# Post-norm Mamba layer with gated feed-forward on one core: mean and variance from channel halves, joined on GpSimd instead of VectorE

## The chip, the cores and the metric

The kernel runs on one core of a Trainium2 chip. Its time is the device time of one execution in microseconds (us); lower is better. The engines are TensorE (PE in the profile, its weight loads PEld), VectorE (DVE), ScalarE (ACT), GpSimd (POOL) and SyncE (SP, which only issues DMAs here).

## The reference

Input x is 8 sequences of 1024 tokens with 256 channels, in float32. One layer is computed, a Mamba block and then a gated feed-forward, each followed by a residual sum and a layer norm without weights:

```
def _layernorm(x, axis=-1, eps=1e-05):
    m = jnp.mean(x, axis=axis, keepdims=True)
    v = jnp.var(x, axis=axis, keepdims=True)
    return (x - m) / jnp.sqrt(v + eps)
...
    xz = jnp.einsum('bld,ed->ble', x, W_in); xi, z = jnp.split(xz, 2, axis=-1)
    u = silu(xc + conv_b)                       # xc: causal convolution of xi, 4 taps
    dt = softplus(W_dt of the first 16 rows of W_xproj u, plus b_dt)
    h = h * exp(dt A) + (dt * u) B;  y = sum over the 16 states of h C
    y = (y + u * D_skip) * silu(z);  out = W_out y
x = _layernorm(x + mamba(x))
x = _layernorm(x + w_down(silu(w_gate x) * (w_up x)))
```

The einsums of the feed-forward use int32 weights divided by 127. The middle lines are the reference's loops written short.

## The kernel before

**Chunks.** The tokens are handled in 16 chunks of 512 (two per sequence). The inner 512 channels are 4 blocks of 128 partitions, with 16 states each, so a chunk has 64 scans (`scan`, L846, VectorE), each over 512 tokens of one channel block and one state. The chunks overlap in a software pipeline: during the scans of chunk k the engines also do the input projection, convolution and `dt` of chunk k+1 ("head") and the output projection, first norm, feed-forward and second norm of chunk k-1 or k-2 ("tail"). Each engine has its own program. The side work is put between the scans by tables written out by hand, keyed by (quad of four scans, place in the quad): `PE_SIDE`, `ACT_SIDE`, `DVE_SIDE`, `POOL_SIDE`, and `*_LAST`, `*_END` for the last chunk. All order between engines comes from semaphores.

**What feeds the scans.** A scan reads a decay (ScalarE, `decay_step`, L641, into one of three PSUM banks) and a drive. GpSimd makes the drives: `drive_unit` (L512) multiplies `dtu` with two rows of B in one instruction of 128x1024 elements; a chunk has 32 such units, unit j feeds scans 2j and 2j+1, and there are four buffers, so unit j waits for the end of scan 2(j-4)+1 (L501). TensorE transposes the states of a finished quad (`transposes`, L1075), ScalarE copies them out (`evacuate`, L648), and TensorE sums over states (L1089).

**Side work that this case touches.**
- Convolution (`conv`, L867, VectorE): three instructions per channel block, each reads two SBUF tensors (`xi` and `acc`). Table entry (2, 2) does block 0, behind scan 10; entry (5, 0) does blocks 1 to 3 with the first half of the first norm's sums, `("r1", 0)`, ahead of the last two.
- `clamp` (L875, a one-input VectorE instruction on 128x1024) and `softplus_max` (L881, two SBUF inputs) make `dt`.
- `add_and_stats` (L883 to L896, VectorE), twice per norm and chunk: the residual sum, `bn_stats` for two blocks of 128 tokens, a wait for the first of these, a throwaway memset, and `bn_aggr` for the two blocks. The places are (5, 0) and (5, 2) for the first norm, (15, 1) and (15, 3) for the second.
- `scale_and_shift` (L545 to L554, GpSimd), once per norm and chunk: from `mv` it makes `rstd` and `shift`. Table items `("std", 0)` at (6, 1), behind drive unit 13, and `("std", 1)` at (0, 1), behind unit 1. Units 14 and 15, `gate_y` (L527) and `dt_times_u` (L543) stand behind the first.
- `normalise` (L707, ScalarE) waits for the fourth of these steps and applies both.
- `heads` (L532, GpSimd) waits for the last convolution of the chunk, ahead of units 12 and 13.
- Products of TensorE go through two PSUM banks in turn (`RING`, L166): `room` (L1115) makes a product wait until the product two before it has been read. In the feed-forward the readers are VectorE's `gate_silu` (L901) and `hidden` (L906).

The first norm's steps run in 15 chunks (1 to 15), those of the second in 14 (2 to 15), and once more at the end. The last chunk's tail has its own code (`end_norm`, L995) with `bn_aggr` on VectorE, which the change leaves alone.

Of the kernel before, what the change touches and what calls it, by code (L numbers as in the profile page):

```python
# [18 lines left out]
P = 128  # L19
T = 512  # L20
TB = T // P
# [4 lines left out]
DM = 256  # L26
# [8 lines left out]
EPS = 1e-5  # L35
# [6 lines left out]
ALU = mybir.AluOpType  # L42
# [154 lines left out]
def wait(eng, sem, value):  # L197

    if not isinstance(value, int) or value > 0:
        eng.wait_ge(sem, value)  # L200
# [60 lines left out]
def mamba_ffn(nc, x, xT, W_inT, conv_w, conv_b, W_xT, W_dtT, b_dt, A_log, D_skip, W_outT,  # L261
# [5 lines left out]
    with ExitStack() as ctx:  # L267
        def sb(name, shape, dt=F32):
            return ctx.enter_context(nc.sbuf_tensor(name, shape, dt))
# [4 lines left out]
        def sem(name):  # L274
            return ctx.enter_context(nc.semaphore(name))
# [17 lines left out]
        eps = sb("eps", [P, TB])  # L293
        minus = sb("minus", [P, TB])
        spare = sb("spare", [P, 1])
# [19 lines left out]
        stats = sb("stats", [P, 2, TB, 6])  # L315
        mv = sb("mv", [P, 2, TB, 2])
        var = sb("var", [P, 2, TB])
        rstd = sb("rstd", [P, 2, TB])
        shift = sb("shift", [P, 2, TB])
        spare_g = sb("spare_g", [P, TB])  # L320
# [11 lines left out]
        def bank(k, what, i):  # L332
            return ring[place[what, i, k.index] % RING]
# [44 lines left out]
        g_n = [sem("g_n1"), sem("g_n2")]  # L378
# [114 lines left out]

        @block.gpsimd
        def _(eng):
            tt = nc.gpsimd.tensor_tensor

            def drive_unit(k, j, first=False):

# [44 lines left out]

            def scale_and_shift(k, norm):  # L545

                wait(eng, (v_s1, v_s2)[norm], k.count(8, 8))
                wait(eng, (a_x1, a_o)[norm], k.count(4, 0))
                tt(var[:, norm, :], mv[:, norm, :, 1], eps[:, :], ALU.add).then_inc(g_n[norm], 1)
                tt(shift[:, norm, :], mv[:, norm, :, 0], minus[:, :], ALU.mult).then_inc(g_n[norm], 1)  # L550
                eng.wait_ge(g_n[norm], k.count(4, 1))
                tt(rstd[:, norm, :], var[:, norm, :], half_neg[:, :], ALU.pow).then_inc(g_n[norm], 1)
                eng.wait_ge(g_n[norm], k.count(4, 3))
                tt(shift[:, norm, :], shift[:, norm, :], rstd[:, norm, :], ALU.mult).then_inc(g_n[norm], 1)  # L554

            def item(k, what, i, tail, head, late, first):
                if what == "end_std":
                    scale_and_shift(k + -1, 1)
                if what == "gate":
                    if i < CB - 1:  # L560
                        gate_y(k, i)
                    elif not first:
                        gate_y(k + -1, i)
                if what == "std" and (late if i else tail):
                    scale_and_shift(k + (-2 if i else -1), i)
                if what == "diag" and i == 0 and head:
                    diagonals(k + 1, 0)
                if what == "diag" and i > 0 and not first:
                    diagonals(k, i)
                if what == "heads" and head:  # L570
                    heads(k + 2)
                if what == "dtu":
                    if i == 0 and head:
                        dt_times_u(k + 1, 0)
                    if i == 1:
                        dt_times_u(k, 1)
# [53 lines left out]
        def _(eng):  # L630
# [71 lines left out]

            def normalise(k, norm, done):

                wait(eng, g_n[norm], k.count(4, 4))
                for tb in range(TB):
                    act(res[:, k.parity, tb, :], res[:, k.parity, tb, :], ACT.Identity, scale=rstd[:, norm, tb:tb + 1],  # L707
                        bias=shift[:, norm, tb:tb + 1]).then_inc(done, 1)
# [7 lines left out]
            def item(k, what, i, tail, head, late, first, *more):  # L716
# [29 lines left out]
                if what == "norm" and (late if i else tail):  # L746
                    normalise(k + (-2 if i else -1), i, (a_x1, a_o)[i])
# [63 lines left out]
            def end_item(k, what, *of):  # L811
                if what == "end_hT":
                    evacuate(k, *of)
                if what == "end_y":
                    copy_y(k, CB - 1)
                if what == "end_norm":
                    normalise(k + -1, 1, a_o)
                if what == "end_x1T":
                    end_x1T(k, *of)
                if what == "end_tanh":  # L820
                    end_tanh(k, *of)
# [7 lines left out]
        def _(eng):  # L829
            tt, ts, stt = nc.vector.tensor_tensor, nc.vector.tensor_scalar, nc.vector.scalar_tensor_tensor  # L830
# [52 lines left out]
            def add_and_stats(k, i, norm, ready, what, done, stat):  # L883

                wait(eng, ready, k.count(2, i + 1))
                if norm == 0 and i == 0:
                    wait(eng, l_res, k.count(16, 16))
                two = res[:, k.parity, 2 * i:2 * i + 2, :]
                tt(two, bank(k, what, i)[:, :].rearrange("p (a d) -> p a d", a=2), two, ALU.add).then_inc(done, 1)
                eng.wait_ge(done, k.count(2, i + 1))  # L890
                for tb in (2 * i, 2 * i + 1):
                    nc.vector.bn_stats(stats[:, norm, tb, :], res[:, k.parity, tb, :]).then_inc(stat, 1)
                eng.wait_ge(stat, k.count(8, 4 * i + 2))
                nc.vector.memset(spare[:, :], 0.0)
                for tb in (2 * i, 2 * i + 1):
                    nc.vector.bn_aggr(mv[:, norm, tb, :], stats[:, norm, tb, :]).then_inc(stat, 1)  # L896

            def gate_silu(k, m):

# [8 lines left out]
            def rest_of_layer(k, what, i):  # L908
                if what == "r1":
                    add_and_stats(k, i, 0, p_out, "out", v_r1, v_s1)  # L910
                if what == "gs":
                    gate_silu(k, i)
                if what == "hid":
                    hidden(k, i)
                if what == "r2":
                    add_and_stats(k, i, 1, p_down, "down", v_r2, v_s2)
# [456 lines left out]
```

## Time and profile before

| | us |
|---|---|
| median of 3 runs | 1891.04 (1888.94 to 1891.07) |
| profiled execution, own time | 1891.66 |
| its span, first to last instruction | 1889.7 |
| busy PE / DVE / ACT / POOL | 1763.2 / 1708.9 / 1656.7 / 1498.0 |
| granted TensorE clock, mean | 0.984 |

A chunk of the steady part takes 112.7 to 112.8 us. Read the table with this in mind: four engines are busy for 79% to 93% of the span, and which of them sets the pace changes several times within a chunk. The share of an engine over the whole span says little; one chunk has to be read piece by piece. Chunk 9 (1049.2 to 1162 us) is read in the rows below.

### The profile page before, as it was taken

The page shows a single profiled execution, that of the slowest core. Times are in us where ns is not written, and L with a number is a line of the kernel's source. Part 1 is how long each engine was busy: PE and PEld are TensorE (multiplying, and loading weights), DVE is VectorE, ACT ScalarE, POOL GpSimd, SP SyncE. Part 2 cuts the span into 40 slices and gives each one's busy share as a digit, 9 for nine tenths or more (in the row PEclk, how much of TensorE's full clock was granted, in tenths as well). Part 3 has the DMA queues.
Part 4 walks back from the last instruction along what each step waited for, and adds up shares of the span by engine and source line. Part 5 has one row for each costly group of instructions (what it writes and reads, how often), then busy time and mean ns, then how long its engine had stood idle before and what let it go on. Part 6 is the DMA issues. An engine that isn't in the chain of part 4 may idle for free.

```text
span 1889.7 us, 40293 instructions
## 1 busy us (share of the span) xinstructions
PE 1763.2 (93%) x15674; PEld 1218.9 (65%) x15674; DVE 1708.9 (90%) x1946; ACT 1656.7 (88%) x2892; POOL 1498.0 (79%) x847
## 2 busy tenths in 40 slices
PE   6577999999999999999999999999999999999997
PEld 2354666766667666666766667676666766667676
DVE  5789999999999999999999999999999999999874
ACT  5688989899898998989899898989989899898961
POOL 2797887879888797987879878787988879888850
PEclk9798999999999999999999999999999999999999
DMA  6030121201312012121201313121131301212000
GB/s 200 1 82 34 4 112 14 97 28 3 123 4 112 14 39 87 3 112 15 112 14 2 123 3 113 15 87 37 4 123 4 113 14 24 102 20 84 24 1 23
DMA packets 171341, 100.55 MB, mean 53 GB/s; under 512 B 139392, under 2 KB 157568, under 8 KB 162960
## 3 DMA queue, kind: packets, MB, share of 16 engines
q1 hardware_dynamic: 171152, 97.98, 17.8%
q8 instruction: 124, 2.03, 0.4%
q14 instruction: 65, 0.53, 0.1%
HBM read 88.52 MB, written 9.44 MB: 52 GB/s over the span
## 4 chain that ended last, share of the span: by engine, by line
PE 48%; ACT 17%; DVE 17%; issue 11%; POOL 6%; DMA 0%; ACTq 0%; DVEq 0%; POOLq 0%
PE ring L1096 19%; PE tp L1075 14%; DVE h L846 8%; PE yb L1089 7%; ACT decay L641 6%; DVE acc L867 5%; ACT hT L648 5%; PE ring L1184 4%; POOL drive L512 3%; ACT acc L657 2%; ACT xi L659 1%; POOL diag_c L521 1%; ACT yt L669 1%; PE decay L1293 1%; ACT dt L695 1%
## 5 line engine op out<-in xcount | busy, mean ns | idle before, releaser
L512 POOL TENSOR_TENSOR drive<-dtu,b_all 128x1024 f32<-128x1024 f32 x512 | 1223.9, 2422 | 91.6 <-DVE h L846 78.8
L641 ACT ACTIVATE decay<-dt,a_neg 128x512 f32<-128x512 f32 x1024 | 707.8, 712 | 81.7 <-DVE h L846 80.6
L648 ACT ACTIVATE hT<-tp 128x512 f32<-128x512 f32 x1024 | 594.4, 611 | 81.9 <-PE tp L1075 80.8
L1075 PE MATMUL tp<-ident,h 128*128 128x128 f32 x4096 | 584.7, 280 | 80.5 <-ACT hT L648 71.0
L846 DVE TENSOR_TENSOR_SCAN h<-decay,h,drive 128x512 f32<-128x512 f32 x512 | 624.6, 1269 | 37.6 <-ACT decay L641 37.6
L846 DVE TENSOR_TENSOR_SCAN h<-decay,drive 128x512 f32<-128x512 f32 x512 | 597.2, 1211 | 61.4 <-ACT decay L641 44.1
L1075 PEld LDWEIGHTS tp<-ident,h 128*128 128x128 f32 x4096 | 465.5, 142 | 288.2 <-issue 140.3
L1089 PE MATMUL yb<-hT,diag_c 128*32 128x128 f32 x8192 | 275.5, 277 | 4.3 <-POOL diag_c L521 2.5
L1089 PEld LDWEIGHTS yb<-hT,diag_c 128*32 128x32 f32 x8192 | 210.7, 110 | 89.0 <-issue 53.2
L1096 PE MATMUL ring<-xt,w_in 128*128 128x512 f32 x512 | 241.9, 606 | 21.7 <-DVE yg L857 16.8
L867 DVE SCALAR_TENSOR_TENSOR acc<-xi,cw,acc 128x512 f32<-128x512 f32 x192 | 169.7, 898 | 14.8 <-ACT xi L659 10.8
L1096 PE MATMUL ring<-xt,w_u 128*128 128x512 f32 x360 | 170.9, 597 | 0.4 <-DVE hid L901 0.4
L1096 PE MATMUL ring<-xt,w_g 128*128 128x512 f32 x360 | 167.4, 594 | 0.0
L1096 PEld LDWEIGHTS ring<-xt,w_in 128*128 128x128 f32 x512 | 91.1, 193 | 109.1 <-issue 84.5
L532 POOL TENSOR_TENSOR spare_g<-eps,minus 128x4 f32<-128x4 f32 x17 | 4.1, 240 | 149.8 <-DVE acc L867 149.7
L527 POOL TENSOR_TENSOR yg<-yg,sz 128x512 f32<-128x512 f32 x63 | 80.8, 1283 | 45.8 <-DVE yg L857 45.8
L1184 PE MATMUL ring<-w_d,xi 128*128 128x256 f32 x480 | 113.5, 379 | 0.0
L1160 PE MATMUL ring<-w_out,yg 128*128 128x256 f32 x480 | 108.6, 379 | 0.0
L1160 PEld LDWEIGHTS ring<-w_out,yg 128*128 128x128 f32 x480 | 88.9, 190 | 11.3 <-issue 0.5
L1184 PEld LDWEIGHTS ring<-w_d,xi 128*128 128x128 f32 x480 | 88.9, 190 | 10.8
L1096 PEld LDWEIGHTS ring<-xt,w_g 128*128 128x128 f32 x360 | 62.4, 190 | 50.4 <-issue 43.0
L1096 PEld LDWEIGHTS ring<-xt,w_u 128*128 128x128 f32 x360 | 61.3, 190 | 46.4 <-issue 45.8
(127 smaller groups left out, 1598.3 us busy)
## 6 DMA issues: line engine op xcount, KB each, us to landing
b_all<-bc_scratch SPq DMA_DIRECT2D x64, 1024.0 KB, 9.3
xt<-in_xT SPq DMA_DIRECT2D x16, 512.0 KB, 4.6
res<-in_x SPq DMA_DIRECT2D x16, 512.0 KB, 13.8
out<-res SPq DMA_DIRECT2D x15, 512.0 KB, 2.9
c_col<-bc_scratch SPq DMA_DIRECT2D x256, 2.0 KB, 2.4
bc_scratch<-dbl SPq DMA_DIRECT2D x16, 64.0 KB, 1.6
w_g<-in_w_gT SPq DMA_DIRECT2D x1, 768.0 KB, 6.8
w_u<-in_w_uT SPq DMA_DIRECT2D x1, 768.0 KB, 7.1
```

The lines of the kernel that those rows point to most:

```text
L512: tt(drive[:, j % 4, :, :], src, b_all[:, n:n + 2, :], ALU.mult).then_inc(g_dr, 1)
L527: tt(yg[:, cb, :], yg[:, cb, :], sz[:, cb, :], ALU.mult).then_inc(g_y, 1)
L641: act(decay[decay_slot(k.parity, i)][:, :], dt[:, cb, :], ACT.Exp, scale=a_neg[:, cb, n:n + 1]).then_inc(a_da, 1)
L648: act(hT[:, (64 * k.index + g) % HTS, :], tp[g % 2][:, :], ACT.Copy).then_inc(a_ev, 1)
L657: act(acc[:, cb, :], bank(k, "xi", cb)[:, :], ACT.Identity, scale=cw[:, cb, KW - 1:KW], bias=cbias[:, cb:cb + 1]).then_inc(a_xi, 1)
L846: nc.vector.tensor_tensor_scan(h[:, h_slot(k.parity, q), at:at + T, i % 4], decay[decay_slot(k.parity, i)][:, :], drive[:, (i // 2) % 4, i ...
L867: stt(acc[:, cb, :], xi[:, cb, tap:tap + T], cw[:, cb, tap:tap + 1], acc[:, cb, :], ALU.mult, ALU.add).then_inc(v_conv, 1)
L1075: last = nc.tensor.transpose(tp[g % 2][:, b * P:(b + 1) * P], h[:, h_slot(k.parity, q), t0:t0 + TS, :].rearrange("p t s -> p (t s)"), iden ...
L1089: last = mm(yb[b * TS:(b + 1) * TS, f * P:(f + 1) * P], diag_c[:, q % 4, 4 * f + b, :], hT[:, (64 * k.index + g) % HTS, b * P:(b + 1) * P] ...
L1096: last = mm(bank, lhsT, rhs, start=i == 0, stop=i == len(pairs) - 1)
L1160: last = mm(bank(k, "out", i)[:, half * DM:(half + 1) * DM], yg[:, c, tb * P:(tb + 1) * P], w_out[:, c, :], start=c == 0, stop=c == CB - 1)
L1184: last = mm(bank(k, "down", i)[:, half * DM:(half + 1) * DM], hidden_block(m)[:, tb * P:(tb + 1) * P], w_d[:, m, :], start=m == 0, stop=m ...
```

## The change

GpSimd no longer reads `mv` but the raw output of `bn_stats`, which holds for even and for odd channels a count, a mean and the sum of squared differences (elements 1, 2 and 4, 5 are read). It joins them in ten steps of 128x4 elements: difference and sum of the means, sum of the squares, half the difference squared, division by 256, eps, sum, power, and the shift. VectorE loses the wait, the memset and the aggregations in `add_and_stats`. GpSimd's first wait is now for the last `bn_stats`, and ScalarE's `normalise` waits for the tenth step.

```diff
@@ -315,6 +315,7 @@
         stats = sb("stats", [P, 2, TB, 6])
         mv = sb("mv", [P, 2, TB, 2])
         var = sb("var", [P, 2, TB])
+        apart = sb("apart", [P, 2, TB])
         rstd = sb("rstd", [P, 2, TB])
         shift = sb("shift", [P, 2, TB])
         spare_g = sb("spare_g", [P, TB])
@@ -493,7 +494,7 @@
 
         @block.gpsimd
         def _(eng):
-            tt = nc.gpsimd.tensor_tensor
+            tt, ts = nc.gpsimd.tensor_tensor, nc.gpsimd.tensor_scalar
 
             def drive_unit(k, j, first=False):
 
@@ -544,13 +545,24 @@
 
             def scale_and_shift(k, norm):
 
-                wait(eng, (v_s1, v_s2)[norm], k.count(8, 8))
+                means = [stats[:, norm, :, at] for at in (1, 4)]
+                squares = [stats[:, norm, :, at] for at in (2, 5)]
+                wait(eng, (v_s1, v_s2)[norm], k.count(4, 4))
                 wait(eng, (a_x1, a_o)[norm], k.count(4, 0))
-                tt(var[:, norm, :], mv[:, norm, :, 1], eps[:, :], ALU.add).then_inc(g_n[norm], 1)
-                tt(shift[:, norm, :], mv[:, norm, :, 0], minus[:, :], ALU.mult).then_inc(g_n[norm], 1)
-                eng.wait_ge(g_n[norm], k.count(4, 1))
+                tt(apart[:, norm, :], *means, ALU.subtract).then_inc(g_n[norm], 1)
+                tt(var[:, norm, :], *squares, ALU.add).then_inc(g_n[norm], 1)
+                tt(shift[:, norm, :], *means, ALU.add).then_inc(g_n[norm], 1)
+                eng.wait_ge(g_n[norm], k.count(10, 3))
+                tt(apart[:, norm, :], apart[:, norm, :], apart[:, norm, :], ALU.mult).then_inc(g_n[norm], 1)
+                eng.wait_ge(g_n[norm], k.count(10, 4))
+                ts(apart[:, norm, :], apart[:, norm, :], 0.25, EPS, ALU.mult, ALU.add).then_inc(g_n[norm], 1)
+                ts(var[:, norm, :], var[:, norm, :], 1.0 / DM, None, ALU.mult).then_inc(g_n[norm], 1)
+                ts(shift[:, norm, :], shift[:, norm, :], -0.5, None, ALU.mult).then_inc(g_n[norm], 1)
+                eng.wait_ge(g_n[norm], k.count(10, 6))
+                tt(var[:, norm, :], var[:, norm, :], apart[:, norm, :], ALU.add).then_inc(g_n[norm], 1)
+                eng.wait_ge(g_n[norm], k.count(10, 8))
                 tt(rstd[:, norm, :], var[:, norm, :], half_neg[:, :], ALU.pow).then_inc(g_n[norm], 1)
-                eng.wait_ge(g_n[norm], k.count(4, 3))
+                eng.wait_ge(g_n[norm], k.count(10, 9))
                 tt(shift[:, norm, :], shift[:, norm, :], rstd[:, norm, :], ALU.mult).then_inc(g_n[norm], 1)
 
             def item(k, what, i, tail, head, late, first):
@@ -702,7 +714,7 @@
 
             def normalise(k, norm, done):
 
-                wait(eng, g_n[norm], k.count(4, 4))
+                wait(eng, g_n[norm], k.count(10, 10))
                 for tb in range(TB):
                     act(res[:, k.parity, tb, :], res[:, k.parity, tb, :], ACT.Identity, scale=rstd[:, norm, tb:tb + 1],
                         bias=shift[:, norm, tb:tb + 1]).then_inc(done, 1)
@@ -890,10 +902,6 @@
                 eng.wait_ge(done, k.count(2, i + 1))
                 for tb in (2 * i, 2 * i + 1):
                     nc.vector.bn_stats(stats[:, norm, tb, :], res[:, k.parity, tb, :]).then_inc(stat, 1)
-                eng.wait_ge(stat, k.count(8, 4 * i + 2))
-                nc.vector.memset(spare[:, :], 0.0)
-                for tb in (2 * i, 2 * i + 1):
-                    nc.vector.bn_aggr(mv[:, norm, tb, :], stats[:, norm, tb, :]).then_inc(stat, 1)
 
             def gate_silu(k, m):
 
```

GpSimd at `("std", 0)`, place (6, 1) of the table in a chunk. Before, drive units 12 and 13, the four steps and unit 14:

```order
L512 TENSOR_TENSOR drive<-dtu,b_all 128x1024 [waits v_h] x2
L549 TENSOR_TENSOR var<-mv,eps 128x4 [waits a_x1,v_s1]
L550 TENSOR_TENSOR shift<-mv,minus 128x4
L552 TENSOR_TENSOR rstd<-var,half_neg 128x4 [waits g_n1]
L554 TENSOR_TENSOR shift<-shift,rstd 128x4 [waits g_n1]
L512 TENSOR_TENSOR drive<-dtu,b_all 128x1024 [waits v_h]
```

With the change (line numbers moved by one and more; `apart` is the new tile):

```order
L513 TENSOR_TENSOR drive<-dtu,b_all 128x1024 [waits v_h] x2
L552 TENSOR_TENSOR apart<-stats 128x4 [waits a_x1,v_s1]
L553 TENSOR_TENSOR var<-stats 128x4
L554 TENSOR_TENSOR shift<-stats 128x4
L556 TENSOR_TENSOR apart<-apart 128x4 [waits g_n1]
L558 TENSOR_SCALAR apart<-apart 128x4 [waits g_n1]
L559 TENSOR_SCALAR var<-var 128x4
L560 TENSOR_SCALAR shift<-shift 128x4
L562 TENSOR_TENSOR var<-var,apart 128x4 [waits g_n1]
L564 TENSOR_TENSOR rstd<-var,half_neg 128x4 [waits g_n1]
L566 TENSOR_TENSOR shift<-shift,rstd 128x4 [waits g_n1]
L513 TENSOR_TENSOR drive<-dtu,b_all 128x1024 [waits v_h]
```

Six instructions are added between unit 13 and unit 14, and four waits on the engine's own semaphore stand where two did. The same ten stand at `("std", 1)` between units 1 and 2.

VectorE in the convolution burst of place (5, 0), before:

```order
L867 SCALAR_TENSOR_TENSOR acc<-xi,cw,acc 128x512 [waits a_xi]
L889 TENSOR_TENSOR res<-ring,res 128x512 [waits l_res,p_out]
L892 BN_STATS stats<-res 128x6 [waits v_r1]
L892 BN_STATS stats<-res 128x6
L894 MEMSET spare 128x1 [waits v_s1]
L896 BN_AGGR mv<-stats 128x2 x2
L867 SCALAR_TENSOR_TENSOR acc<-xi,cw,acc 128x512 [waits v_conv] x2
```

With the change:

```order
L879 SCALAR_TENSOR_TENSOR acc<-xi,cw,acc 128x512 [waits a_xi]
L901 TENSOR_TENSOR res<-ring,res 128x512 [waits l_res,p_out]
L904 BN_STATS stats<-res 128x6 [waits v_r1]
L904 BN_STATS stats<-res 128x6
L879 SCALAR_TENSOR_TENSOR acc<-xi,cw,acc 128x512 [waits v_conv] x2
```

The memset and both aggregations are gone between the `bn_stats` pair and the last two convolutions; the other three places of `add_and_stats` lose the same three instructions.

## Rows read from the trace of the kernel before

**Rows 1.** Windows table of chunk 9: stretch, its length, busy us by engine
```profile
1070.00:1097.00 27.00, 24.01 (x207) 17.67 (x208) 26.67 (x32) 25.94 (x48) 14.47 (x10) 1.00 0.06 21
1105.00:1130.00 25.00, 25.00 (x223) 15.55 (x224) 21.94 (x22) 23.18 (x43) 25.00 (x12) 1.00 0.19 3
1130.00:1162.00 32.00, 32.00 (x301) 23.50 (x302) 31.96 (x34) 27.76 (x47) 26.11 (x13) 1.00 0.28 102
```

**Rows 2.** Groups by line: form, count | busy us, mean ns | idle before
```profile
L892 DVE BATCH_NORM_STATS2 stats<-res 128x6 f32<-128x256 f32 x120 | 45.2, 418 | 2.1
L534 POOL COPY xi<-xi 128x12 f32<-128x12 f32 x8 | 2.3, 286 | 0.0
```

**Rows 3.** Timeline of VectorE in the second convolution burst (start us, us)
```profile
1094.21 0.75 DVE L892 BATCH_NORM_STATS2 stats<-res 128x6 f32<-128x256 f32 x2
1095.16 1.51 DVE L867 SCALAR_TENSOR_TENSOR acc<-xi,cw,acc 128x512 f32<-128x512 f32 x2
```

**Rows 4.** Timeline of GpSimd, first norm and drives behind it
```profile
1102.73 0.20 POOL L549 TENSOR_TENSOR var<-mv,eps 128x4 f32<-128x4 f32 x1
1102.88 0.20 POOL L550 TENSOR_TENSOR shift<-mv,minus 128x4 f32<-128x4 f32 x1
1103.03 1.00 POOL L552 TENSOR_TENSOR rstd<-var,half_neg 128x4 f32<-128x4 f32 x1
1104.11 0.20 POOL L554 TENSOR_TENSOR shift<-shift,rstd 128x4 f32<-128x4 f32 x1
1104.26 2.39 POOL L512 TENSOR_TENSOR drive<-dtu,b_all 128x1024 f32<-128x1024 f32 x1
1110.16 2.40 POOL L512 TENSOR_TENSOR drive<-dtu,b_all 128x1024 f32<-128x1024 f32 x1
```

**Rows 5.** Timeline of VectorE, scan 28, scans 30 and 31, a ring evacuation
```profile
1109.07 1.28 DVE L846 TENSOR_TENSOR_SCAN h<-decay,h,drive 128x512 f32<-128x512 f32 x1 [1.84 <-ACT decay L641]
...
1112.81 2.47 DVE L846 TENSOR_TENSOR_SCAN h<-decay,h,drive 128x512 f32<-128x512 f32 x2 [0.30 <-ACT decay L641]
...
1123.04 0.67 DVE L906 TENSOR_TENSOR xi<-ring,xi 128x512 f32<-128x512 f32 x1
```

**Rows 6.** Timeline of TensorE, the product that waits for that evacuation
```profile
1123.88 1.88 PE L1096 MATMUL ring<-xt,w_g 128*128 128x512 f32 x4
```

**Rows 7.** Timeline of ScalarE, the normalisation of the first norm
```profile
1105.89 2.07 ACT L707 ACTIVATE res<-res,shift,rstd 128x256 f32<-128x256 f32 x4
```

**Rows 8.** Timeline around the second norm: VectorE clamp, GpSimd var
```profile
1054.49 0.66 DVE L875 TENSOR_SCALAR dt<-acc 128x1024 f32<-128x1024 f32 x1
...
1054.66 0.56 POOL L549 TENSOR_TENSOR var<-mv,eps 128x4 f32<-128x4 f32 x1 [0.75 <-DVE mv L896]
```

**Rows 9.** Timeline of VectorE, softplus maximum to first convolution
```profile
1060.14 2.21 DVE L881 TENSOR_TENSOR dt<-acc,dt 128x1024 f32<-128x1024 f32 x1
...
1066.79 2.46 DVE L846 TENSOR_TENSOR_SCAN h<-decay,h,drive 128x512 f32<-128x512 f32 x2 [0.89 <-ACT decay L641]
1069.65 2.46 DVE L846 TENSOR_TENSOR_SCAN h<-decay,h,drive 128x512 f32<-128x512 f32 x2 [0.40 <-ACT decay L641]
1072.02 2.43 DVE L867 SCALAR_TENSOR_TENSOR acc<-xi,cw,acc 128x512 f32<-128x512 f32 x1
...
1074.49 1.54 DVE L867 SCALAR_TENSOR_TENSOR acc<-xi,cw,acc 128x512 f32<-128x512 f32 x2
```

**Rows 10.** Timeline of GpSimd, drives 7 and 8 of that chunk
```profile
1069.18 2.40 POOL L512 TENSOR_TENSOR drive<-dtu,b_all 128x1024 f32<-128x1024 f32 x1
...
1071.51 2.40 POOL L512 TENSOR_TENSOR drive<-dtu,b_all 128x1024 f32<-128x1024 f32 x1
```

**Rows 11.** List of waits: who <- whom: total us, times, longest
```profile
DVE h L846 <- POOL drive L512: 12.1, 3, 8.9
```

**Rows 12.** Timelines of the first chunk: VectorE convolutions, GpSimd drives
```profile
60.37 8.13 DVE L867 SCALAR_TENSOR_TENSOR acc<-xi,cw,acc 128x512 f32<-128x512 f32 x3
...
60.07 7.88 POOL L512 TENSOR_TENSOR drive<-dtu,b_all 128x1024 f32<-128x1024 f32 x3
```

## Prediction

> **What bounds the kernel now.** I read the engines' busy shares, then the chain that ended last, then a table of stretches and the timelines of chunk 9, the other chunks only to see that they repeat it. The shares say that TensorE is fullest; the stretches say more. From 1105 to 1162 us TensorE is busy for 57 of 57 us, so nothing that ends sooner on another engine is worth anything there; but VectorE has 31.96 of 32 in the second part of it, so what comes late on VectorE stays late [rows 1]. From 1070 to 1097 it is VectorE that has no room, 26.67 of 27, while GpSimd works for 14.47 and TensorE for 24.01 [rows 1]. So a microsecond counts in full on VectorE ahead of the last convolution, and on TensorE behind 1105. GpSimd is never full over a chunk, but what it makes at two places decides when the full engines can go on.
>
> **What VectorE gives back.** Each of the four calls per chunk loses two aggregations and a memset. Behind the `bn_stats` pair, which ends at 1094.21 + 0.75 = 1094.96, the next convolution starts at 1095.16; the second of two neighbours starts some 0.09 ahead of the first one's end (two of 0.42 [rows 2] make a pair of 0.75), so without the aggregations it would start at 1094.87: 0.29 us per call [rows 3]. Of the four calls only the one at (5, 0) lies in the stretch that VectorE sets, and it lies ahead of the last convolution, for which the activation of u and GpSimd's `heads` wait. It is in 14 chunks (1 to 14): 14 x 0.29 = 4.1 us. The call at (5, 2) is followed by scans that wait for decays, the one behind the second down product only ends where VectorE waits for ScalarE a little later (0.89 us at 1066.79, [rows 9]), and the one at (15, 1) is followed by a wait for TensorE. These three I cost at nothing; if all of them counted it would be 60 x 0.29 = 17.4 us.
>
> **What the ten steps cost on GpSimd.** A step that depends on nothing new starts 0.15 behind the one before (1102.73 to 1102.88), has its result 0.20 after its start, and one that waits for a result starts 0.08 behind its end (1104.03 to 1104.11) [rows 4]. The four steps take 1102.73 to 1104.26, 1.53 us. The ten: starts at 0, 0.15 and 0.30; the square waits for the third, 0.50 + 0.08 = 0.58; its scaling 0.58 + 0.28 = 0.86; two more at 1.01 and 1.16; the sum at 1.31; the power at 1.31 + 0.28 = 1.59; it takes 1.00, so the last step starts at 2.67 and the next drive at 2.82. That is **1.29 us more** per call. A two-constant TENSOR_SCALAR of GpSimd on 128x4 is not in this trace. From below it is as cheap as the TENSOR_TENSOR steps (0.15 apart); from above it is as dear as the power, 1.00 us [rows 4], which would make three steps 2.5 us dearer. The nearest plain row, a copy of 12 elements, has 0.29 [rows 2]; so I take the cheap end and keep 0.1 each, 0.3 a call, as the likely excess. The Trainium skill says on its page Perfetto Trace Analysis (section GPSIMD Engine Instruction) that GpSimd should be timed from start to start and not by the durations shown. By the durations the six added steps would be 6 x 0.20 = 1.20 us, by the starts it is 1.29; the sum goes by the starts.
>
> **First norm, place (6, 1).** Behind the steps stand unit 14, the gating of y, `dtu` and unit 15. Unit 15 now ends at 1110.16 + 2.40 = 1112.56, and scan 30, which reads it, starts at 1112.81 [rows 4, 5]. Scan 30 waits for a decay as well (0.30), so 0.25 us is all the cover there is. With 1.29 more, unit 15 ends at 1113.85 and scan 30 starts about 1113.9: VectorE is 1.1 us late. Unit 14 has cover enough: it ends at 1106.65 and scan 28 reads it at 1109.07, since that waits for a decay. What waits for VectorE next? TensorE, at its two banks. `hidden` ends at 1123.71 and the third gate product, which takes its bank's turn, starts at 1123.88 [rows 5, 6]. With 0.06 for the signal (an estimate, no more than the 0.08 of GpSimd's own) that is 0.11 us of slack. So TensorE is late by 1.1 - 0.11 = 1.0 us, and it is full to the end of the chunk. ScalarE's `normalise` starts at 1105.89, when it reaches it; the last step would end at 1102.73 + 2.67 + 0.20 = 1105.60 [rows 4, 7]: covered by 0.2, so here 0.3 us more of excess begins to cost, too. `v_conv`, from which all this runs, comes 0.29 earlier for every engine, so the distances hold. In 14 chunks (1 to 14): 14 x 1.0 = 14.0 us. If this cover were larger than it looks, this term would go to 0; with the 0.3 of excess it is 18.
>
> **Second norm, place (0, 1).** The ten steps stand behind unit 1. They may begin 0.29 earlier, since the last aggregation falls away; the clamp that holds up the first step (it starts at 1054.66 and ends only with the clamp's 1055.15, [rows 8]) comes earlier by the same. So the drives behind are late by 1.29 - 0.29 = 1.0 us. No scan waits there: in the whole trace scans wait for drives three times, 12.1 us, all in the first chunk [rows 11]. What counts is who meets them. An instruction with two SBUF inputs on VectorE does not run beside a drive: the `softplus_max` at 1060.14 takes 2.21, the convolution at 1072.02 takes 2.43 and ends 0.54 behind drive 8 (1073.91), while the two behind it, with GpSimd idle, take 0.77 apiece [rows 9, 10]. When both engines have work, they alternate: in the first chunk three convolutions and three drives take 8.13 and 7.88 us, 2.7 each in turn [rows 12]. The Trainium skill, page SBUF — State Buffer, section Who interferes with whom, calls this an exclusive hold of a shared port pair, in which the second to come is blocked to the end of the first; the trace agrees (0.77 alone, 2.7 in turn), and by the rule moving work from VectorE to GpSimd is no relief where the two meet.
>
> Now shift the drives by 1.0. The `softplus_max` waits for the end of unit 3, 1.0 later; the scans behind it have 0.89 and 0.40 us of waiting to absorb it [rows 9], so the first convolution still comes at 1072.02. Drive 7 ends at 1071.58 + 1.0 = 1072.58 and is in its way; it ends at 1073.12 (behind the drive by 0.54), before drive 8 rather than after it. Drive 8 has waited since 1072.5 and comes next: in turn it takes 2.7 - 0.54 = 2.17 from there, to 1075.29. The second convolution stands behind it to 1075.83, and the third ends at 1076.62, where before it was 1074.49 + 1.54 = 1076.03. VectorE is full from here to 1097: **0.6 us later** per chunk, in 13 chunks (2 to 14): 7.8 us. By both ends: with the excess of 0.3 it is 0.9 x 13 = 11.7; at nothing, if drive 8 were to meet nobody.
>
> **Sum.** 14.0 + 7.8 - 4.1 = 17.7 us on the profiled execution's own 1891.66. That one lies 0.6 above the median of the runs, so the median is 1891.0 + 17.7, rounded to **1909 us**. The last chunk has another table and may give or take 1 us.
>
> **Rivals.**
> - *Only one of the two losses is real.* For it: each hangs on tenths of a microsecond in one chunk's rows. Then 7.8 - 4.1 = 3.7 or 14.0 - 4.1 = 9.9: 1895 or 1901 us.
> - *The steps are dearer.* TENSOR_SCALAR at 0.4 rather than 0.15 makes the call 0.75 longer, in 27 places: 17.7 + 20 = 38, and ScalarE's `normalise` is late as well: 1929 us or more. For it: the power shows that a function may cost five times a sum.
> - *Faster: the three convolutions slip in ahead of drive 8.* Place: 1073.12. If VectorE keeps its turn through all three, they end at 1073.12 + 1.54 = 1074.66, 1.4 ahead of now, and GpSimd's drive 9 is not asked for yet. 13 x -1.4 + 14.0 - 4.1 = -8.3: 1883 us. It decides whether the second convolution, 0.04 us behind the first, is asked for before the waiting drive gets its turn. Against it: the first chunk's alternation [rows 12].
> - *Faster: both delays are absorbed*, by idle time that the rows don't resolve. Then VectorE's 4.1 us are left, at most 17.4: 1874 to 1887 us. Against it: 57 of 57 us [rows 1].
> - *No change:* one small loss against the gain.
>
> **How the numbers follow.** The forecast 0.60, one loss only 0.12, dearer steps 0.10, turn kept 0.07, absorbed 0.06, no change 0.05. So slower by over 0.2% (about what a measurement of this kernel can tell) is 0.82, within 0.2% 0.05, faster 0.13. The range has to leave out the two fast cases and the far end of the dear one: 1889 (no change) to 1928. The forecast's own range is 1902 to 1918 (terms of 10 to 18 and 5 to 12).
>
> **What would show it.** GpSimd's first small step to the next drive 2.8 us, not 1.5; scan 30 waiting for the drive instead of the decay in chunks 1 to 14; the first of the convolutions at (2, 2) shorter than now (about 1.1), the second long (2.7); steady chunks 1.3 us longer than 112.75. Wrong would be: small steps of 0.3 us or more, a convolution trio that is short, or a chunk no longer than before although scan 30 is late, which would mean that TensorE has slack behind 1105.

## The result, and the profile after

| | before | after |
|---|---|---|
| median (lowest to highest), us | 1891.05 (1888.94 to 1891.48, 4 runs) | 1927.31 (1923.34 to 1927.67, 4 runs) |
| profiled execution, its span | 1891.66, 1889.7 | 1927.67, 1925.9 |
| granted TensorE clock, mean | 0.984 | 0.977 |

The ratio is 1.0193 [1.0181, 1.0205]: 36.3 us slower. The forecast was 17.7 slower; the sign was right, the forecast size about half of the measured one, and 1927 lies at the upper end of the range (1928). A steady chunk took 111.9 and 112.8 us in turn before (112.7 to 112.8 is every second one), and takes 113.3 to 116.1 now.

First the page's busy time by engine, after. VectorE has 11.7 us less to do than before, GpSimd 41 more; TensorE has 21 more although it does the same instructions.

```profile
PE 1784.4 (93%) x15674; PEld 1226.7 (64%) x15674; DVE 1697.2 (88%) x1766; ACT 1660.9 (86%) x2892; POOL 1539.3 (80%) x1027
```

The timeline of GpSimd after, first norm of chunk 9 (start us, us). It answers to [rows 4].

```profile
1122.52 0.20 POOL L552 TENSOR_TENSOR apart<-stats 128x4 f32<-128x4 f32 x1
1122.68 0.20 POOL L553 TENSOR_TENSOR var<-stats 128x4 f32<-128x4 f32 x1
1122.83 0.20 POOL L554 TENSOR_TENSOR shift<-stats 128x4 f32<-128x4 f32 x1
1123.11 0.20 POOL L556 TENSOR_TENSOR apart<-apart 128x4 f32<-128x4 f32 x1
1123.39 0.19 POOL L558 TENSOR_SCALAR apart<-apart 128x4 f32<-128x4 f32 x1
1123.66 0.23 POOL L559 TENSOR_SCALAR var<-var 128x4 f32<-128x4 f32 x1
1123.86 0.22 POOL L560 TENSOR_SCALAR shift<-shift 128x4 f32<-128x4 f32 x1
1124.04 0.20 POOL L562 TENSOR_TENSOR var<-var,apart 128x4 f32<-128x4 f32 x1
1124.32 1.04 POOL L564 TENSOR_TENSOR rstd<-var,half_neg 128x4 f32<-128x4 f32 x1
1125.43 0.20 POOL L566 TENSOR_TENSOR shift<-shift,rstd 128x4 f32<-128x4 f32 x1
1125.59 2.38 POOL L513 TENSOR_TENSOR drive<-dtu,b_all 128x1024 f32<-128x1024 f32 x1
```

From the first step to the drive it is 3.07 us, 1.54 more than before. Three starts lie further apart than the forecast had them: behind the scaling of `apart` the next starts 0.27 later and not 0.15, then 0.20 and 0.18.

Scan 30 waits for its drive now, where it waited 0.30 for a decay in [rows 5]. The next rows, still of chunk 9, are VectorE, GpSimd, TensorE and ScalarE at that place.

```profile
1133.97 2.46 DVE L858 TENSOR_TENSOR_SCAN h<-decay,h,drive 128x512 f32<-128x512 f32 x2 [1.68 <-POOL drive L513]
...
1131.48 2.38 POOL L513 TENSOR_TENSOR drive<-dtu,b_all 128x1024 f32<-128x1024 f32 x1
...
1136.48 0.65 PE L1083 MATMUL tp<-ident,h 128*128 128x128 f32 x4 [0.75 <-DVE h L858]
...
1144.83 1.98 PE L1104 MATMUL ring<-xt,w_g 128*128 128x512 f32 x4
...
1125.67 2.08 ACT L719 ACTIVATE res<-res,shift,rstd 128x256 f32<-128x256 f32 x4
```

The drive ends at 1133.86, scan 30 starts 0.11 behind it. Scans 30 and 31 end at 1136.43, and 0.05 behind them TensorE starts the transposes of their states, for which it has stood still for 0.75 us. The third gate product ([rows 6]) follows the work before it without idle time, here as before the change. ScalarE's normalisation begins 0.04 behind the last step: covered, as before, but with nothing to spare.

The first convolutions behind scan 10, chunk 9, on VectorE and GpSimd, answer to [rows 9, 10].

```profile
1091.14 1.40 DVE L879 SCALAR_TENSOR_TENSOR acc<-xi,cw,acc 128x512 f32<-128x512 f32 x1
1092.58 2.73 DVE L879 SCALAR_TENSOR_TENSOR acc<-xi,cw,acc 128x512 f32<-128x512 f32 x1
1095.35 0.75 DVE L879 SCALAR_TENSOR_TENSOR acc<-xi,cw,acc 128x512 f32<-128x512 f32 x1
...
1089.64 2.36 POOL L513 TENSOR_TENSOR drive<-dtu,b_all 128x1024 f32<-128x1024 f32 x1
1091.96 2.81 POOL L513 TENSOR_TENSOR drive<-dtu,b_all 128x1024 f32<-128x1024 f32 x1
```

Drive 7 ends at 1092.00 and the first convolution 0.54 behind it, at 1092.54; then drive 8 has its turn to 1094.77, and the second convolution ends 0.54 behind that. This is the turn-taking that the forecast drew. Before, the first took 2.43 and the other two 1.54, and they ended sooner.

And now what it did not draw. TensorE behind that place, chunk 8 and then chunk 9, and the windows table of chunk 8 (stretch, length, busy by engine, granted clock, DMA share, GB/s):

```profile
982.23 0.66 PE L1083 MATMUL tp<-ident,h 128*128 128x128 f32 x4
984.99 2.66 PE L1104 MATMUL ring<-xt,w_in 128*128 128x512 f32 x4 [2.10 <-DVE yg L869]
987.44 1.92 PE L1083 MATMUL tp<-ident,h 128*128 128x128 f32 x8
...
1100.34 1.98 PE L1104 MATMUL ring<-xt,w_in 128*128 128x512 f32 x4 [2.30 <-DVE yg L869]
1102.16 1.04 PE L1083 MATMUL tp<-ident,h 128*128 128x128 f32 x8
```

```profile
982.90:985.00 2.10, 0.01 (x1) 0.01 (x1) 2.10 (x4) 1.84 (x5) 2.10 (x2) 1.00 0.18 64
986.20:989.60 3.40, 3.40 (x11) 2.27 (x10) 3.40 (x4) 2.09 (x4) 3.40 (x3) 0.50 0.00 0
```

In chunk 8 TensorE stands still for 2.1 us, and 1.2 us after it has begun again its granted clock is 0.50 (1.2 GHz) for 3.4 us; eight transposes take 1.92 instead of 1.04. Such a fall stands in nine chunks (3, 4, 6, 7, 8, 10, 11, 12, 14). It begins between 0.2 us before the end of the wait (chunk 6) and 1.4 us behind it (chunk 12). Chunks 2, 5, 9 and 13 have the same wait of 2.1 or 2.3 us, and there the clock stays at 1.00. Before, no steady chunk has such a fall. The wait itself grew. In the list of waits (who <- whom: total, times, longest), before:

```profile
PE ring L1096 <- DVE yg L857: 16.8, 14, 1.4
```

and after:

```profile
PE ring L1104 <- DVE yg L869: 29.3, 14, 2.3
DVE h L858 <- POOL drive L513: 32.5, 17, 9.0
DVE res L901 <- PE ring L1168: 9.1, 10, 1.1
```

The first of the three kinds of wait is for `skip` (`yg`), which stands behind the convolutions on VectorE; a product of TensorE waits for it to free its bank. The second is [rows 11] with 14 waits more: scan 30 in thirteen chunks and one scan of the last chunk. In chunk 2 the profile names the decay, but scan 30 starts 0.10 behind its drive there too. The third had been 2 times, 2.1 us: with TensorE slow, the output product is not ready when VectorE wants to add it, in the middle of the last convolutions. Nine of its ten waits are in the nine chunks with a fall.

### The profile page after: what moved, and what is told of

The parts are those of the page before. It is cut to its first block and busy times, and to the rows that moved or that the text cites. A ratio compares the mean times of both kernels' runs of the same rounds, so it can differ in the third digit from the quotient of the medians.

```text
span 1925.9 us, 40293 instructions
## 1 busy us (share of the span) xinstructions
PE 1784.4 (93%) x15674; PEld 1226.7 (64%) x15674; DVE 1697.2 (88%) x1766; ACT 1660.9 (86%) x2892; POOL 1539.3 (80%) x1027
## 5 line engine op out<-in xcount | busy, mean ns | idle before, releaser
L1104 PE MATMUL ring<-xt,w_in 128*128 128x512 f32 x512 | 254.1, 631 | 35.6 <-DVE yg L869 29.3
L879 DVE SCALAR_TENSOR_TENSOR acc<-xi,cw,acc 128x512 f32<-128x512 f32 x192 | 182.6, 966 | 14.5 <-ACT xi L671 10.4
```

The lines of the kernel that those rows point to most:

```text
L879: stt(acc[:, cb, :], xi[:, cb, tap:tap + T], cw[:, cb, tap:tap + 1], acc[:, cb, :], ALU.mult, ALU.add).then_inc(v_conv, 1)
L1104: last = mm(bank, lhsT, rhs, start=i == 0, stop=i == len(pairs) - 1)
```

## The experiments

Each time stands beside runs of the kernel before on the same chip (medians 1890.8 to 1891.4); behind it stand the ratio to them and its 95% interval.

**1. VectorE's half alone.** No aggregations, and four steps on raw elements of `stats`; mean and variance of the joined halves are left out.

```diff
+                if norm in (0, 1):
+                    tt(var[:, norm, :], squares[0], eps[:, :], ALU.add).then_inc(g_n[norm], 1)
+                    tt(shift[:, norm, :], means[0], minus[:, :], ALU.mult).then_inc(g_n[norm], 1)
...
+                    return
```

> VectorE's half alone: aggregations, memset and their wait are gone, GpSimd keeps four steps in both norms, but they read elements of the raw statistics, so the norms are scaled wrongly. My account: only the call in the convolution burst counts on VectorE (14 x 0.29 = 4 us), and the drives behind the second norm come 0.29 earlier, which the convolution at (2, 2) gets (13 x 0.29 = 4): 1883 to 1887 us. Rival, that every call counts: 60 x 0.29 = 17 us, 1874. Rival, that the removal itself did the harm by shifting phases: above 1895.

Measured 1883.96, 0.9962 [0.9948, 0.9977]: 7.1 us faster. Chunk periods 111.2 and 112.5 us in turn, before 111.9 and 112.8.

**2. GpSimd's half alone.** Ten steps, and the wait, memset and aggregations kept, their results unread.

```diff
-                wait(eng, (v_s1, v_s2)[norm], k.count(4, 4))
+                wait(eng, (v_s1, v_s2)[norm], k.count(8, 8))
```

> GpSimd's half alone: the ten steps in both norms, while VectorE keeps its aggregations (their result is not read) and GpSimd waits for them as before. My account: the steps take 1.54 us more per call by the trace after; at the first norm TensorE is late by about 1.25 x 14 = 17, at the second VectorE's convolutions by 1.2 x 13 = 16, and TensorE's clock falls once in at least 9 chunks (12 us): 1936 us or a little more, slower than the full change. Rival, that the missing aggregations took part in the loss: no slower than 1927.

Measured 1936.08, 1.0247 [1.0224, 1.0270], as expected. The loss is GpSimd's, and VectorE's removed work pays about 9 us of it back in the full change. TensorE's wait is 2.2 to 2.3 us here, and nine steady chunks have a fall of the clock, not quite the same ones.

**3, 4. Ten steps at one norm only.** As experiment 1, with the ten steps kept at the first norm (3) or at the second (4), the other norm reading raw elements.

```diff
-                if norm in (0, 1):
+                if norm in (1,):
```

In experiment 4 it is `(0,)`. The diff is against experiment 1.

> Aggregations gone, ten steps in the first norm only, four in the second (which read raw elements, so that norm is scaled wrongly). My account: 1885 for the common part, plus 14 x 1.25 = 17: about 1902 us, no fall of TensorE's clock in the steady chunks, because the convolutions at (2, 2) and the skip behind them are not late. Rival, that the first norm's lateness is hidden and all of the loss comes from the second: 1885.

> Aggregations gone, ten steps in the second norm only, four in the first (which read raw elements, so that norm is scaled wrongly). My account: 1887 plus 13 x 0.98 = 13 for the convolutions at (2, 2), plus 12 for about nine falls of the clock right behind TensorE's wait for the skip: about 1912 us, with the falls at 26 us into a chunk. Rival, that the clock falls for another reason: 1900 without falls. Together with the run of the first norm alone the losses should add up to that of the full change, within 3 us.

The third gave 1899.69, 1.0048 [1.0032, 1.0065], the fourth 1904.25, 1.0075 [1.0060, 1.0090]. The lists of waits, of the third and then the fourth:

```profile
DVE h L866 <- POOL drive L513: 23.9, 10, 9.0
PE ring L1112 <- DVE yg L877: 13.7, 14, 1.1
```

```profile
PE ring L1112 <- DVE yg L877: 29.2, 14, 2.3
DVE h L866 <- POOL drive L513: 13.5, 4, 9.0
```

So the scans' waits belong to the first norm, TensorE's long wait to the second. (In the even chunks of the third run the profile names the decay, but scan 30 starts 0.10 behind its drive there too.) The first norm costs 1899.7 - 1884.0 = 15.7 us. The fourth has the long wait, 2.1 to 2.3 us, in all of chunks 2 to 14, but only three steady falls of the clock (chunks 6, 10 and 14, of 114.1 instead of 112.4 us), where I had expected nine. Six falls at 1.0 to 1.7 us are 6 to 10 us, which fits the 8 us by which it came out lower. The losses do not add up as I had expected: over experiment 1 they are 15.7 and 20.3, together 36.0, and the full change loses 43.4. The missing 7.3 us are of the size of those six falls too.

**5, 6. `skip` 3 ahead of the first convolutions**, in the changed kernel (5) and in the kernel before (6).

```diff
-    (3, 1): [("skip", 3)],
-    (2, 2): [("conv", 0, 0), ("conv", 0, 1)],
+    (2, 2): [("skip", 3), ("conv", 0, 0), ("conv", 0, 1)],
```

> The full change, with the skip of channel block 3 put ahead of the late convolutions at (2, 2) instead of behind scan 13, so that TensorE's z product no longer waits for it (2.1 us in the trace after). Nothing is made cheaper on VectorE or GpSimd. My account: the falls of TensorE's clock in the steady chunks go away and with them 10 to 12 us: about 1916 us; the convolutions and the drives stay as late as in the full change. Rival, that the clock falls because of the load or for no reason in this wait: falls stay, 1925 or more. Rival, that the wait of TensorE itself also cost time: below 1912.

> The kernel before with the same move of the skip. It has no fall of the clock in the steady chunks and VectorE sets the pace in that stretch, so my account is no change: 1889 to 1892 us. Rival, that TensorE's wait of 1.1 us there counted by itself: 1880 or less.

The fifth: 1908.57, 1.0093 [1.0078, 1.0108], no wait for `yg` in steady chunks and no fall. It takes 18.7 us off the changed kernel, where I had expected 10 to 12, and the sixth tells of a second gain: 1883.54, 0.9959 [0.9945, 0.9973], 7.9 us faster than before where I had expected nothing. VectorE in chunk 8, before and then with the early `skip`:

```profile
959.90 4.07 DVE L867 SCALAR_TENSOR_TENSOR acc<-xi,cw,acc 128x512 f32<-128x512 f32 x3
```

```profile
956.45 0.72 DVE L856 SCALAR_TENSOR_TENSOR yg<-u,dsk,ring 128x512 f32<-128x512 f32 x1
957.09 3.43 DVE L866 SCALAR_TENSOR_TENSOR acc<-xi,cw,acc 128x512 f32<-128x512 f32 x3
```

`skip` takes its 0.65 us out of time in which the convolution would only have waited for a drive: the three end 0.64 sooner from their own start, and at the same distance from scan 0 (20.80 us), with `skip` already done. With the early `skip` TensorE's wait for it is gone as well; that this part gains nothing in the sixth is not shown by itself. The sixth is the fastest version that computes the whole layer (the first leaves a part out).

**7, 8. Second norm's steps moved** from (0, 1) to (4, 0) on GpSimd, behind the convolutions, and ScalarE's second normalisation from (2, 2) to (3, 2), in the kernel before (7) and the changed one (8).

```diff
-    (0, 1): [("std", 1)], (4, 1): [("diag", 1)], (5, 0): [("diag", 2)],
+    (4, 0): [("std", 1)], (4, 1): [("diag", 1)], (5, 0): [("diag", 2)],
...
-    (2, 2): [("hT", 4), ("hT", 5), ("norm", 1)], (2, 3): [("hT", 6), ("hT", 7)], (3, 0): [("z", 1)],
+    (2, 2): [("hT", 4), ("hT", 5)], (2, 3): [("hT", 6), ("hT", 7)], (3, 0): [("z", 1)],
...
+                if what == "std" and i == 1 and late and head:
+                    wait(eng, v_conv, (k + 1).count(12, 3))
```

> The kernel before with the second norm's four steps on GpSimd moved from behind unit 1 to behind unit 8, where GpSimd idles 3.4 us, and made to wait for the third convolution so that they don't meet it; ScalarE's normalisation of that norm moves from (2, 2) to (3, 2). My account: drives 2 to 8 come about 2 us earlier, the first convolution no longer waits for a drive, and VectorE gains 1.0 to 1.8 us per chunk in 13 chunks: 1868 to 1878 us. Rival, that the port between the two engines is not what holds up the convolutions: 1890.

> The full change with the same move of the second norm's ten steps. GpSimd does as much work as in the full change, only later. My account: the convolutions at (2, 2) are no longer late and the clock doesn't fall; what is left is the first norm's loss, as in the run with ten steps there alone (1900 us), less the gain of the freed convolutions (up to 20), plus up to 1.7 us a chunk because the chain of drives behind unit 8 now runs into the second burst of convolutions: 1885 to 1900 us. Rival, that the loss follows GpSimd's busy time wherever the steps stand: 1925.

Both missed: 1896.86, 1.0034 [1.0022, 1.0046], and 1914.37, 1.0123 [1.0108, 1.0138]. One part of the eighth came as expected: TensorE stands still for at most 0.83 us around that place, and no steady chunk has a fall. In the seventh the convolutions ended 1.4 us sooner, but without the wait of the steps GpSimd runs its drives through the start of the chunk, and the clamp meets them. VectorE and GpSimd in the seventh, chunk 9:

```profile
1054.07 2.31 DVE L877 TENSOR_SCALAR dt<-acc 128x1024 f32<-128x1024 f32 x1
...
1051.15 4.68 POOL L512 TENSOR_TENSOR drive<-dtu,b_all 128x1024 f32<-128x1024 f32 x2
```

The clamp takes 2.31 where [rows 8] has 0.66 (2.73 in chunk 8). GpSimd's wait for the statistics had been what kept the way free.

**9. The wait filled.** The changed kernel, with the transposes of group 8, ahead of the long wait, done three times over.

```diff
-                for b in range(4):
+                for b in [0, 1, 2, 3] * (1 + (g == 8) * 2):
```

> The full change, but TensorE repeats the four transposes of group 8 twice more (same data, same bank) just ahead of the z product that waits for the skip, so that about 1.3 us of its wait are filled with work. The skip stays late. My account, that the clock falls because TensorE idles 2.1 us there: no falls in the steady chunks and 10 to 12 us back, 1915 to 1918 us, while the run with the early skip got 7 us more from the skip standing in the convolution's wait. Rival, that the falls come from elsewhere or that the filled wait only moves the delay to ScalarE's copy: 1925 or more.

Measured 1913.54, 1.0119 [1.0104, 1.0134]: useless work on TensorE makes the kernel 13.8 us faster. TensorE in chunk 8 of this run:

```profile
978.21 1.53 PE L1083 MATMUL tp<-ident,h 128*128 128x128 f32 x12
980.96 1.98 PE L1104 MATMUL ring<-xt,w_in 128*128 128x512 f32 x4 [1.22 <-DVE yg L869]
982.78 1.04 PE L1083 MATMUL tp<-ident,h 128*128 128x128 f32 x8
```

The product starts as late in the chunk as in the changed kernel (25.82 us behind scan 0, without the filling 25.83), so VectorE's delay is untouched. What is gone is the fall, in every steady chunk, and the periods are 113.3 and 115.0 us: those that the changed kernel has in its chunks 2, 5, 9 and 13, without a fall. What is left of the wait is 1.2 us in even and 1.4 in odd chunks. Over all the profiles read here the steady falls go with the long wait: they stand only in those of the changed kernel and of experiments 2 and 4, where it is 2.1 to 2.3 us; in the ten others TensorE stands still for at most 1.4 us there, and none has a steady fall.

**10, 11, 12. Clamp kept clear.** Experiment 7 with one wait more, so that unit 2 stands behind the clamp (10); that with the early `skip` (11); all three edits on the changed kernel (12).

```diff
+    (0, 1): [("let_clamp", 1)],
+                if what == "let_clamp" and late:
+                    wait(eng, v_mn, k.count(2, 2))
```

> The kernel before with the second norm's steps moved behind unit 8, as in the earlier run, and unit 2 made to wait for the clamp at the chunk's start. In the earlier run the clamp took 2.3 and 2.7 us instead of 0.66, since with the steps gone from there it met unit 2. My account: the clamp is 0.7 again, the drives are still 1.3 earlier than in the kernel before, the convolutions at (2, 2) gain 1.0 to 1.4 us in 13 chunks: 1873 to 1879 us. Rival, that the later normalisation of that norm costs too: 1885 or more.

> The same with the skip of channel block 3 ahead of the convolutions at (2, 2) too. My account: the skip fills the rest of the convolution's wait, a few tenths of a us per chunk: 1868 to 1876 us. Rival, that the two gains are the same one (both fill the same wait): as the run without the early skip.

> The full change with the same three edits. The second norm's ten steps stand in GpSimd's idle time. My account: what is left over the same edits on the kernel before is the first norm's 16 us less VectorE's 4 to 7, plus up to 1.3 us a chunk where the later drives run into the second convolution burst: 1882 to 1900 us. Rival, that the ten steps cost as much wherever they stand: 1905 or more.

1889.15, 0.9992 [0.9983, 1.0002]; 1887.19, 0.9980 [0.9971, 0.9990]; 1906.70, 1.0083 [1.0068, 1.0098]. All three missed. For the tenth only times are at hand. The clamp is back at 0.66 us in the eleventh, but the convolutions gain 0.5 us instead of 1.4, and `softplus_max`, 2.21 in [rows 9], now meets the drives for longer:

```profile
1056.41 3.23 DVE L884 TENSOR_TENSOR dt<-acc,dt 128x1024 f32<-128x1024 f32 x1
```

None came out lower than experiment 6. The eleventh and the twelfth differ by 19.5 us. The first norm's 15.7, less VectorE's half (4 to 7 us), leave 8 to 11 us for the second norm's steps, not much less than in their old place: the rival, 1905 or more, had the number. What they do there shows at the second convolution burst of chunk 8, the eleventh and then the twelfth:

```profile
971.34 5.30 DVE L870 SCALAR_TENSOR_TENSOR acc<-xi,cw,acc 128x512 f32<-128x512 f32 x7
```

```profile
980.70 6.47 DVE L882 SCALAR_TENSOR_TENSOR acc<-xi,cw,acc 128x512 f32<-128x512 f32 x7
```

The longer steps push the drives behind them into this burst, where one convolution takes 1.64 us instead of 0.75.

## Why the prediction was half right

The runs split the 36.3 us, each step by medians (in another order the shares could differ by a few us): before to 1 is VectorE's half, 1 to 3 the first norm, 3 to 9 the second without falls (with the filling, which leaves the periods of fall-free chunks as they are), 9 to the changed kernel the falls.

| | forecast | measured |
|---|---|---|
| VectorE's half | -4.1 and, at the second norm, -0.29 x 13 = -3.8 | -7.1 |
| ten steps, first norm | 14.0 | 15.7 |
| ten steps, second norm | 7.8 + 3.8 = 11.6 | 13.9 |
| clock of TensorE | none | 13.8 |
| sum | 17.7 | 36.3 |

(The forecast set the second norm's 0.29 off within its own term; it stands apart here.)

**VectorE's half: right.** In experiment 1 the burst at (5, 0) is 0.27 us shorter, for 0.29 forecast, and the last convolution, counted from scan 0, ends 0.53 (chunk 8) and 0.29 us (chunk 9) earlier. The chunks are 0.66 and 0.34 us shorter, 0.50 on average, for a forecast of 0.58. That the other two places gave nothing follows from this sum; no run took them apart.

**The ten steps: 1.54, not 1.29.** The price of a TENSOR_SCALAR was the open bound; it was 0.18 to 0.27 between starts, not the 0.15 of its neighbours. Most of the 0.3 of excess that I named as likely was there, and the sum had left it out. To time by starts held: the durations of all steps add up to 1.28 us more than before, the starts to 1.54.

**First norm: mechanism right, place not.** Scan 30 starts 0.10 behind its drive in chunks 1 to 14, as said. But TensorE is stopped at the transposes of those states, at 1136.48, and not at the bank of the third gate product. The forecast had 0.11 us of slack at that bank, but the trace before shows no wait there: TensorE was at work up to the product's start. In experiment 3 against 1 scan 30 is 1.31 and 1.43 us late (forecast 1.1) and the third gate product is 0.96 (chunk 8) and 1.22 us (chunk 9) late, where 1.0 was forecast.

**Second norm: mechanism right, size short.** The alternation came: 1.40, 2.73, 0.75 where about 1.1 and 2.7 were forecast. Counted from scan 0 the three end 0.98 us later than before in chunk 8 and 1.22 in chunk 9 (forecast 0.6). Against experiment 1, where the aggregations are gone as well, it is 1.24 and 1.25, for a forecast of 0.9; 0.25 of the rest is that of the steps, the remaining 0.1 is not explained. `softplus_max` did not wait for the later unit 3: it slipped in ahead of it and took 1.20 us instead of 2.21, but behind it the scans wait for decays, and the first convolution came no sooner.

**The step that failed is what comes behind the late convolutions.** The forecast ended with "0.6 us later per chunk", as VectorE being full. It did not ask who waits for VectorE's next instruction, `skip`. TensorE did, 14 times 1.2 us already, and its wait became 2.1. The wait by itself shows no price: from experiment 3 to 9 the convolutions end 1.17 and 1.24 us later and the chunks grow by 1.11 and 1.20, so VectorE's lateness accounts for all of it. It cost 13.8 us by the clock that fell, a term that the forecast had at nothing. Of the rivals none had it. "Dearer steps" had a number near the result (1929), by another way: its price for a step was 0.4, measured are 0.18 to 0.27, and `normalise` was not late. Experiment 9 decides: all else was left as it was, transposes were put into the front of the wait, and the 13.8 us came back (whether by the shorter wait or by their being work, it does not tell). The profiles agree: against the same chunk of experiment 9 one with a fall is 1.04 to 1.07 us (odd chunks, as 116.07 against 115.03) or 1.36 to 1.47 (even, as 114.76 against 113.29) longer, over 3 and 6 chunks 11.8 us, of 12.0 between the two spans, 1925.9 - 1913.9. The other 5 us by which the forecast fell short are its three terms above, each a little off.

**Open.** Why the same wait makes the clock fall in nine chunks of the changed kernel and in three of experiment 4, but not in chunk 9 of the changed kernel. When the wait comes, counted from the start of the execution, differs from chunk to chunk, but no run varied that alone. The Trainium skill, page TensorE: Matmul & The Clock Gate, section The HAM clock gate, says that the gate's watch on activity runs freely and does not start anew with the kernel. That chunks alike in their work differ agrees with it; it is not shown here.

## What to carry to other kernels

Follow a delay past the engine that you hold for the bound, to every engine that waits for its next instructions, and look for a TensorE wait that grows: up to 1.4 us it was harmless in this kernel, at 2.1 to 2.3 the clock fell in many chunks. Where TensorE has to wait, order what frees its bank ahead of what only stands in line for a port; one moved `skip` gave 18.7 us here and 7.9 in the kernel before. A wait on GpSimd may be what keeps a VectorE instruction clear of it, so look at who runs in the gap before closing it.

## What the runs showed of the hardware

- TensorE's granted clock can fall to half (1.2 GHz) for 3.4 us around a standstill of 2.1 to 2.3 us (busy 0.01 of 2.10 in chunk 8). It did in 9 of the 13 chunks with that standstill, in 9 of 13 in experiment 2 and in 3 of 13 in experiment 4, from 0.2 us before work began again to 1.4 us behind. Three sets of transposes instead of one ahead of the wait, which left 1.2 to 1.4 us of it, avoided the fall in all steady chunks.
- A clamp of one SBUF input, 128x1024 float32, takes 0.66 us alone and 2.31 to 2.73 beside drives of GpSimd. The Trainium skill, page SBUF — State Buffer, section Who interferes with whom, counts `tensor_scalar` among those that can hold the shared port pair; the trace agrees.
- VectorE's convolutions, which read two SBUF tensors, and GpSimd's drives take turns where both have work: three convolutions took 1.40, 2.73 and 0.75 us with drives of 2.4 and 2.8 us between them.
- On GpSimd a 128x4 TENSOR_SCALAR is 0.18 to 0.27 us from the next start, a TENSOR_TENSOR 0.15 to 0.16 from the next start that waits for nothing, and a power 1.04 long.
